# A Mamba block and a routed expert layer on one core: placement earlier on VectorE, ranks earlier on TensorE, the last gate product in halves on GpSimd

## The chip, the core and the metric

The kernel runs on one core of one Trainium2 chip. The metric is the device time of one execution in microseconds (us). Engines are called as in the profile: PE is TensorE (its weight loads are PEld), DVE is VectorE, ACT is ScalarE, POOL is GpSimd, SP is SyncE, which here only issues DMAs.

## The reference

Input x is (2, 2048, 256) in float32, so 4096 tokens of width 256. Two layers follow each other, each with a residual and a layer normalization without scale.

```python
# layer 1: Mamba block without the scan
xz = x @ W_in.T                      # 256 -> 2 * 512: xs, z
xc = silu(causal_depthwise_conv(xs, 4 taps) + conv_b)
dt = xc @ W_x[0:32].T                # 512 -> 32
a  = softplus(dt @ W_dt.T + b_dt)    # 32 -> 512
x  = layernorm(x + (xc * a * silu(z)) @ W_out.T + x)
# layer 2: 16 experts, 4 of them for each token, and a shared expert
scores = sigmoid(x @ gate_w.T); sfc = scores + gate_bias
groups of 4 experts, each rated by its two best sfc; the best 2 of 4 groups stay
topk = the 4 best experts by sfc in the groups that stay
w = 2.5 * scores[topk] / sum(scores[topk])
y = sum over topk of w * (silu(x @ Wg.T) * (x @ Wu.T)) @ Wd.T
y = y + (silu(x @ Ws_g.T) * (x @ Ws_u.T)) @ Ws_d.T
out = layernorm(x + x + y)
```

## The kernel before

**Stages.** The tokens are cut into 8 token tiles of 512. The first stage (to about 300 us of the trace) works through them in a software pipeline. While token tile t has its softplus, output projection and normalization, tile t + 1 has its input projection and convolution, tile t - 1 its gate, routing and shared expert, and tile t - 2 its placement. The second stage (300 to 513 us) runs the experts over 143 list tiles of 128 rows, in 36 groups of four ("quads"). The tail adds the four weighted expert rows of each token and normalizes.

**How a token reaches its experts.** For each token tile DVE finds the four experts of each token (`choose_...`, result `sel`). PE counts, with triangular and all-ones matrices, the rank of each token in each expert's list (`ranks`). DVE then places the tokens: `place_rank` adds the ranks to the counts of the tiles before (two additions), `place_rows` masks them, `place_top` (four MAX8) collects the four positions of each token, and `place_ids` writes the row numbers `row_id` and raises the semaphore `routed`. POOL then sends the rows of the tile to `x_buf` in HBM with indirect DMAs (`send`): four blocks of 128 tokens with four DMAs each, 16 for a token tile. In the second stage SP loads list tiles from `x_buf`, and POOL sends the results to `y_buf` (`send_results`), four indirect DMAs for each quad. POOL works in the order of its program, so the result sends stand behind all row sends.

**POOL's other work.** `gate_product` multiplies the convolved channels `xc` by `silu(z)` for the four chunks of 128 channels of a token tile, into `m`. DVE multiplies `m` by the softplus in halves of two chunks (`softplus_product`), which PE's output projection (`out_proj_by_pairs`) waits for.

**The order on DVE.** All engines run orders that are written out by hand. In `tile(t)` the small routing and placement operations stand between larger ones. `conv_tap(n, c, d)` is one tap of the convolution of chunk c of tile n = t + 1, some 510 columns wide; the taps of one chunk follow each other, each waiting for the one before. `conv_halo(n, i)` adds the columns that reach into the tile before, for chunks 2i and 2i + 1; ACT's `silu_xc` waits for it. The last token tile (t = 7, with p = 5 placed and r = 6 routed) has an order of its own behind the loop, since it has no next tile: no taps, and the table of the first half's list tiles (`table_mm` on PE, `table_out` on DVE). There DVE finishes the weights of token tile 5 first (`weigh_chosen` is the multiplication at line 1688, `slot_chosen` the scan at line 1692, each with two inputs in SBUF), then adds up the gate's logits of tile 6 (`gate_logits`, line 1566, semaphore `gate_sum`).

**Waits that matter.** On PE `ranks(t, logits_read)` waits for `sel_done` of its tile, for `routed` of the tile before it, and for `gate_sum`, because its output shares PSUM bank 3 with the logits that `gate_logits` reads. `place_rank` waits for the ranks. `softplus_sum(7, 0)` waits for ACT's logarithm. `gate_product(7, ...)` waits on POOL for `norm_ready`, which DVE raises at line 1527 (`norm_shift`). SP's load of the expert weights (`load_gu`) waits for all of `m` and stands behind the loads of the first two quads.

Of the kernel before, what the change touches and what calls it, by code (L numbers as in the profile page):

```python
# [22 lines left out]
def mamba_moe(nc, x_tok, x_T, w_in_T, conv_w, conv_b, w_x_T, w_dt_T, b_dt, w_out_T,  # L23
# [9 lines left out]
    SUB = T // P  # L33
    KD, KI, KS = D // P, DI // P, SH // P
# [23 lines left out]
    with ExitStack() as ctx:  # L58
# [539 lines left out]
        def _(pool):  # L598
# [46 lines left out]
            def gate_product(t, chunks):  # L645
                at_least(pool, "wout_mm", 2 * t)
                for c in chunks:
                    at_least(pool, "xc_done", KI * t + c + 1)
                    at_least(pool, "z_evac", KI * t + c + 1)
                    nc.gpsimd.tensor_tensor(m[:, c, :], xc[:, c, :], zs[:, c, :], ALU.mult).then_inc(s["m_done"], 1)  # L650
# [42 lines left out]
            def last_tile(t):  # L693
                send(t - 3, range(1, 2))
                at_least(pool, "norm_ready", t)
                gate_product(t, range(0, KI))
                send(t - 3, range(2, SUB))
                send(t - 2)
                send(t - 1)
                send(t)  # L700
# [30 lines left out]
        def _(pe):  # L731
# [298 lines left out]
            t = NT - 1  # L1030
# [3 lines left out]
            gate_turn(t - 1)  # L1034
            dt_out(t, range(2, KI))
            table_mm(0)
            shared_up(t - 1, 0)
            ranks(t - 2, t)
            out_proj_by_pairs(t)
            shared_up(t - 1, 1)  # L1040
            at_least(pe, "table_done", 2)
# [337 lines left out]
        def _(dve):  # L1379
# [517 lines left out]
            def tile(t, more=True):  # L1897
# [22 lines left out]
                softplus_sum(t, 1)  # L1920
                gate_one(r)
                softplus_product(t, 1)
                gate_score(r)
                conv_tap(n, 1, 1)
                if placed:
                    place_rank(p)
                gate_biased(r)
                conv_tap(n, 1, 2)
                if placed:
                    place_rows(p)  # L1930
                group_pairs(r)
                conv_tap(n, 1, 3)
                if placed:
                    place_top(p)
                group_sums(r)
                conv_halo(n, 0)
                if placed:
                    place_ids(p)
                group_score(r)
                if t < 2:  # L1940
                    weights_low(PIECES_OF[t][0])
                shared_act(r, 0)
# [228 lines left out]
            t = NT - 1  # L2171
# [9 lines left out]
            weights_to_rows(p)  # L2181
            gate_logits(r)
            table_out(0)
            softplus_sum(t, 0)
            softplus_product(t, 0)
            place_rank(p)
            place_rows(p)
            place_top(p)
            softplus_sum(t, 1)
            place_ids(p)  # L2190
            gate_one(r)
            softplus_product(t, 1)
            gate_score(r)
# [148 lines left out]
```

How the kernel before makes its waits and increments, by code:

```python
        def at_least_alone(eng, name, n):  # L237
            if isinstance(n, int):
                return at_least(eng, name, n)
            n = eng.to_reg(n)
            eng.wait_ge(s["ones_ready"], 1)
            eng.wait_ge(s[name], n)
# [1 line left out]
        def at_least(eng, name, n):  # L246
            if isinstance(n, int) and n <= 0:
                return
            eng.wait_ge(s[name], n)
# [346 lines left out]
        @block.gpsimd  # L597
        def _(pool):
            nc.gpsimd.memset(ident[:, :], 0.0).then_inc(s["pool_set"], 1)
            pool.wait_ge(s["pool_set"], 1)
            nc.gpsimd.affine_select(out=ident[:, :], in_=ident[:, :], compare_op=ALU.not_equal, fill=1.0,
                                    base=0, pattern=[[-1, P]], channel_multiplier=1).then_inc(s["id_ready"], 1)
            nc.gpsimd.memset(tri[:, :], 1.0).then_inc(s["pool_set"], 1)
            pool.wait_ge(s["pool_set"], 2)
            nc.gpsimd.affine_select(out=tri[:, :], in_=tri[:, :], compare_op=ALU.is_gt, fill=0.0,
                                    base=0, pattern=[[1, P]], channel_multiplier=-1).then_inc(s["tri_ready"], 1)
            nc.gpsimd.memset(ones[:, :], 1.0).then_inc(s["ones_ready"], 1)
            nc.gpsimd.memset(before[:, :, :], 1.0).then_inc(s["pool_set"], 1)
            pool.wait_ge(s["pool_set"], 3)
            nc.gpsimd.affine_select(out=before[:, :, :], in_=before[:, :, :], compare_op=ALU.is_gt, fill=0.0,
                                    base=0, pattern=[[1, NG], [-1, NG]], channel_multiplier=0) \
```

## Time and profile before

| | us |
|---|---|
| median of 3 runs (lowest to highest) | 550.43 (549.23 to 551.96) |
| the profiled execution's own time | 549.61 |
| its span in the profile | 548.1 |
| PE busy | 516.9 (94%) |
| DVE busy | 412.3 (75%) |
| ACT busy | 376.1 (69%) |
| POOL busy | 327.4 (60%) |

The span is what the trace covers; the rest of the profiled execution's own time (1.5 us) lies around it. Busy shares are means over stages that have different limits. In a timeline row the first number is the start in us from the span's start, the second the time from the first start to the last end of the instructions in the row, and a bracket at its end gives the engine's idle time just before it and what ended it. PE's matmuls overlap, so a row's duration is longer than the step to the next row.

### The profile page before, as it was taken

What the parts mean: (1) busy time and instruction counts of PE and PEld (TensorE: products, weight loads), DVE (VectorE), ACT (ScalarE), POOL (GpSimd) and SP (SyncE); (2) the same over time, 40 slices, a digit from 0 to 9 for tenths busy, and PEclk for the clock granted to TensorE, in tenths of its full rate; (3) what the DMA queues carried; (4) which work ended last, traced back from release to release, by engine and by line L of the source; (5) the groups of instructions that cost most, each with busy time, mean ns of one, the idle gap of its engine ahead of it and who ended that gap; (6) DMA issues with size and microseconds to landing.
All of it is one profiled execution on the core that took longest, in us unless ns stands there. A gap on an engine that the chain in (4) does not pass through costs nothing.

```text
span 548.1 us, 11651 instructions
## 1 busy us (share of the span) xinstructions
PE 516.9 (94%) x3125; PEld 441.7 (81%) x3125; DVE 412.3 (75%) x1097; ACT 376.1 (69%) x961; POOL 327.4 (60%) x361
## 2 busy tenths in 40 slices
PE   5898899999999999999998999999999999999984
PEld 4687486786877868778677899999999999999862
DVE  4887598897997979989796747444354578878964
ACT  4694867949669495692845367778777777777473
POOL 4412013138657486576877777777777777777700
PEclk9999899999999999999999999999999999999996
DMA  6994403224233342312399867986766899997978
GB/s 165 306 260 166 163 38 117 78 83 141 77 140 106 114 142 76 143 65 101 111 328 367 280 223 247 305 257 193 223 197 211 285 301 328 344 320 241 341 234 287
DMA packets 70150, 111.06 MB, mean 203 GB/s; under 512 B 12260, under 2 KB 53477, under 8 KB 69576
## 3 DMA queue, kind: packets, MB, share of 16 engines
q1 hardware_dynamic: 56856, 74.36, 43.3%
q0 software_dynamic: 12672, 35.67, 17.5%
q8 instruction: 29, 0.48, 0.4%
q10 hardware_dynamic: 560, 0.27, 0.2%
q14 instruction: 33, 0.27, 0.2%
HBM read 61.63 MB, written 49.69 MB: 203 GB/s over the span
## 4 chain that ended last, share of the span: by engine, by line
PE 65%; DVE 10%; ACT 7%; DMA 6%; issue 6%; SPq 5%; ACTq 0%; POOL 0%; DVEq 0%; POOLq 0%
PE psum L785 8%; PE psum L726 6%; PE psum L728 6%; PE psum L727 6%; PE psum L760 4%; PE psum L855 4%; DMA tiles_in<-x_buf 4%; PE psum L979 4%; PE psum L981 4%; PE psum L980 4%; PE psum L963 4%; PE psum L1079 3%; SPq L556 2%; PE psum L1003 2%; PE psum L1005 2%
## 5 line engine op out<-in xcount | busy, mean ns | idle before, releaser
L658 POOL DMA_INDIRECT x_buf<-row,row_id x128 | 129.5, 1012 | 51.4 <-issue 35.8
L650 POOL TENSOR_TENSOR m<-xc,zs 128x512 f32<-128x512 f32 x32 | 41.4, 1316 | 93.4 <-DVE shift L1527 55.0
L979 PE MATMUL psum<-ew_gu_hi,t_hi 128*128 x286 | 83.8, 293 | 0.4 <-issue 0.4
L981 PE MATMUL psum<-ew_gu_hi,t_lo 128*128 x286 | 80.9, 283 | 0.0
L980 PE MATMUL psum<-ew_gu_lo,t_hi 128*128 x286 | 80.9, 283 | 0.0
L1449 DVE SCALAR_TENSOR_TENSOR xc<-psum,cw_taps,xc 128x511 f32<-128x511 f32 (+2 forms) x96 | 70.7, 738 | 6.5 <-ACT halo_x L1118 5.1
L715 POOL DMA_INDIRECT y_buf<-y_out,y_ids x56 | 56.9, 1016 | 16.9 <-issue 12.7
L2055 DVE TENSOR_TENSOR e_act<-g_act,psum 128x512 f32<-128x512 f32 x36 | 24.5, 681 | 45.4 <-ACT g_act L1287 41.0
L785 PE MATMUL psum<-wout,m 128*128 128x256 f32 x256 | 57.3, 382 | 1.1 <-DVE m L1484 0.6
L785 PEld LDWEIGHTS psum<-wout,m 128*128 128x128 f32 x256 | 48.0, 190 | 10.0 <-DVE sp L1476 3.1
L726 PE MATMUL psum<-x_hi,win_hi 128*128 128x512 f32 x128 | 53.3, 416 | 2.4 <-issue 1.2
L979 PEld LDWEIGHTS psum<-ew_gu_hi,t_hi 128*128 128x128 f32 x286 | 54.6, 191 | 0.6 <-issue 0.5
L980 PEld LDWEIGHTS psum<-ew_gu_lo,t_hi 128*128 128x128 f32 x286 | 54.8, 192 | 0.0
L981 PEld LDWEIGHTS psum<-ew_gu_hi,t_lo 128*128 128x128 f32 x286 | 54.7, 191 | 0.0
L715 POOL DMA_INDIRECT y_buf<-row,y_ids x40 | 43.3, 1084 | 12.2 <-issue 10.4
L728 PE MATMUL psum<-x_hi,win_lo 128*128 128x512 f32 x128 | 50.3, 393 | 0.0
L727 PE MATMUL psum<-x_lo,win_hi 128*128 128x512 f32 x128 | 50.2, 392 | 0.0
L2046 DVE TENSOR_TENSOR t_lo<-psum,t_hi 128x512 fp32r<-128x512 f32 x72 | 46.3, 683 | 2.3 <-ACT t_hi L1281 2.2
L715 POOL DMA_INDIRECT y_buf<-y_pair,y_ids x40 | 39.5, 987 | 12.2 <-issue 10.7
L1003 PE MATMUL psum<-ew_d_hi,a_hi 128*128 x143 | 43.4, 303 | 1.4 <-ACT y_out L1302 0.6
L2060 DVE TENSOR_TENSOR a_lo<-psum,a_hi 128x512 fp32r<-128x512 f32 x36 | 24.8, 690 | 25.0 <-ACT a_hi L1294 23.7
L1287 ACT ACTIVATE g_act<-psum 128x512 f32<-128x512 f32 x36 | 21.5, 598 | 28.6 <-PE psum L981 28.5
(256 smaller groups left out, 1390.3 us busy)
## 6 DMA issues: line engine op xcount, KB each, us to landing
tiles_in<-x_buf SPq DMA_DIRECT2D x143, 144.0 KB
y_pair<-y_buf SPq DMA_DIRECT2D x20, 512.0 KB
y_in<-y_buf SPq DMA_DIRECT2D x12, 512.0 KB, 7.3
xT<-in_x_T SPq DMA_DIRECT2D x8, 512.0 KB, 4.2
xtok<-in_x_tok SPq DMA_DIRECT2D x8, 512.0 KB, 3.6
gu_hi_buf<-w_hi_now SPq DMA_DIRECT2D x8, 512.0 KB, 3.4
x_buf<-pad_row SPq DMA_DIRECT2D x17, 144.0 KB
raw_gu<-in_wg_T SPq DMA_DIRECT2D x16, 128.0 KB, 3.4
```

The costliest lines, as they stand in the source:

```text
L658: nc.gpsimd.indirect_dma_start(out=x_buf, out_offset=bass.IndirectOffsetOnAxis(ap=row_id[t % ROWS][:, b, k:k + 1], axis=0), in_=row[t % RO ...
L715: nc.gpsimd.indirect_dma_start(out=y_buf, out_offset=bass.IndirectOffsetOnAxis(ap=y_ids[:, q % IDS, i:i + 1], axis=0), in_=y_sent[:, i, :] ...
L726: pe.matmul(o, w_hi, v_hi, start=start, stop=False)
L727: pe.matmul(o, w_hi, v_lo, start=False, stop=False)
L728: return pe.matmul(o, w_lo, v_hi, start=False, stop=stop)
L785: mm = pe.matmul(o, m[:, c, b * P:(b + 1) * P], wout[:, c, :], start=c == 0 and b % 2 == 0, stop=c == KI - 1 and b % 2 == 1)
L979: pe.matmul(o, t_hi[par][:, k, r], w_hi, start=k == 0, stop=False)
L980: pe.matmul(o, t_hi[par][:, k, r], w_lo, start=False, stop=False)
L981: mm = pe.matmul(o, t_lo[par][:, k, r], w_hi, start=False, stop=k == KD - 1)
L1003: pe.matmul(o, a_hi[:, r], w_hi, start=True, stop=False)
L1449: V.scalar_tensor_tensor(xc[:, c, d:T], psum[:, x_bank(c), 0:T - d], taps[:, c, HALO - d:HALO - d + 1], xc[:, c, d:T], ALU.mult, ALU.add). ...
L2046: V.tensor_tensor(t_lo[par][:, k, :], x_turned(q, k), f32(t_hi[par][:, k, :]), ALU.subtract) \
```

## The change

Three orders are changed, and no operation is added or removed. On POOL the last token tile's gate product, four multiplications in a row until now, is cut into two halves, with the four sends of one block of token tile 4 between them. On PE, in the last token tile, the rank matmuls of token tile 5 go ahead of the shared expert's first product. On DVE, in the loop's `tile(t)`, the placement of tile t - 2 no longer alternates with the taps of chunk 1 but with the routing operations ahead of them, and the halo addition follows the third tap. In the last token tile `place_rank` and `place_rows` go ahead of `softplus_sum(7, 0)`, `place_top` between it and `softplus_product(7, 0)`, and `place_ids` behind that product.

```diff
--- before.py
+++ after.py
@@ -693,8 +693,10 @@
             def last_tile(t):
                 send(t - 3, range(1, 2))
                 at_least(pool, "norm_ready", t)
-                gate_product(t, range(0, KI))
-                send(t - 3, range(2, SUB))
+                gate_product(t, range(0, 2))
+                send(t - 3, range(2, 3))
+                gate_product(t, range(2, KI))
+                send(t - 3, range(3, SUB))
                 send(t - 2)
                 send(t - 1)
                 send(t)
@@ -1034,8 +1036,8 @@
             gate_turn(t - 1)
             dt_out(t, range(2, KI))
             table_mm(0)
+            ranks(t - 2, t)
             shared_up(t - 1, 0)
-            ranks(t - 2, t)
             out_proj_by_pairs(t)
             shared_up(t - 1, 1)
             at_least(pe, "table_done", 2)
@@ -1920,23 +1922,23 @@
                 softplus_sum(t, 1)
                 gate_one(r)
                 softplus_product(t, 1)
-                gate_score(r)
-                conv_tap(n, 1, 1)
                 if placed:
                     place_rank(p)
-                gate_biased(r)
-                conv_tap(n, 1, 2)
+                gate_score(r)
                 if placed:
                     place_rows(p)
-                group_pairs(r)
-                conv_tap(n, 1, 3)
+                gate_biased(r)
                 if placed:
                     place_top(p)
-                group_sums(r)
-                conv_halo(n, 0)
+                group_pairs(r)
                 if placed:
                     place_ids(p)
+                conv_tap(n, 1, 1)
+                group_sums(r)
+                conv_tap(n, 1, 2)
                 group_score(r)
+                conv_tap(n, 1, 3)
+                conv_halo(n, 0)
                 if t < 2:
                     weights_low(PIECES_OF[t][0])
                 shared_act(r, 0)
@@ -2181,13 +2183,13 @@
             weights_to_rows(p)
             gate_logits(r)
             table_out(0)
-            softplus_sum(t, 0)
-            softplus_product(t, 0)
             place_rank(p)
             place_rows(p)
+            softplus_sum(t, 0)
             place_top(p)
+            softplus_product(t, 0)
+            place_ids(p)
             softplus_sum(t, 1)
-            place_ids(p)
             gate_one(r)
             softplus_product(t, 1)
             gate_score(r)
```

## Rows read from the trace of the kernel before

**Rows 1.** Busy time by stretch of the trace: start:end, length, busy us (instructions), clock, DMA.

```profile
166.00:200.00 34.00, 34.00 (x154) 26.09 (x153) 29.90 (x91) 23.72 (x44) 22.41 (x26) 1.00 0.34 115
...
340.00:500.00 160.00, 158.03 (x1340) 156.53 (x1340) 96.83 (x170) 122.83 (x443) 123.14 (x122) 1.00 0.82 273
```

**Rows 2.** DVE timeline, token tile 4: start us, us, instruction.

```profile
178.37 0.55 DVE L1575 RECIPROCAL score<-sfc 128x64 f32<-128x64 f32 x1
...
181.89 0.15 DVE L1463 TENSOR_TENSOR xc<-xc,halo 128x6 f32<-128x6 f32 x1
181.97 0.16 DVE L1756 TENSOR_SCALAR row_id<-top 128x16 int32<-128x16 f32 x1
...
191.89 2.31 DVE L1449 SCALAR_TENSOR_TENSOR xc<-psum,cw_taps,xc 128x511 f32<-128x511 f32 x3
```

**Rows 3.** DVE timeline, token tile 6, end of its normalization.

```profile
260.11 0.16 DVE L1527 SCALAR_TENSOR_TENSOR shift<-mv,rstd 128x4 f32<-128x4 f32 x1
```

**Rows 4.** POOL timeline before the last token tile, with idle time before each.

```profile
251.14 0.96 POOL L658 DMA_INDIRECT x_buf<-row,row_id  x1 [1.85 <-DVE row_id L1756]
...
261.00 2.52 POOL L650 TENSOR_TENSOR m<-xc,zs 128x512 f32<-128x512 f32 x2
```

**Rows 5.** POOL timeline, last token tile.

```profile
264.30 2.50 POOL L650 TENSOR_TENSOR m<-xc,zs 128x512 f32<-128x512 f32 x2 [0.77 <-ACT xc L1129]
...
277.98 1.70 POOL L658 DMA_INDIRECT x_buf<-row,row_id  x1 [0.30 <-DVE row_id L1756]
```

**Rows 6.** DVE timeline, token tiles 6 and 7: instructions while POOL multiplies.

```profile
263.13 0.42 DVE L1463 TENSOR_TENSOR xc<-xc,halo 128x6 f32<-128x6 f32 x1
...
266.46 0.39 DVE L1797 SCALAR_TENSOR_TENSOR list_step<-list_size,list_step 128x31 f32<-128x31 f32 x1
```

**Rows 7.** DVE timeline, last token tile.

```profile
268.22 0.68 DVE L1468 TENSOR_TENSOR dt<-psum,dt 32x512 fp32r<-32x512 f32 x1
268.93 0.23 DVE L1688 TENSOR_TENSOR equal<-score,sel 128x64 f32<-128x64 f32 x1
269.08 0.28 DVE L1692 TENSOR_TENSOR_SCAN picked<-ones_f,sel 128x64 f32<-128x64 f32 x1
...
271.60 0.28 DVE L1566 TENSOR_REDUCE score<-psum 128x64 f32<-128x128 f32 x1
...
273.08 1.23 DVE L1476 SCALAR_TENSOR_TENSOR sp<-psum,sp 128x1024 f32<-128x1024 f32 x1 [0.86 <-ACT sp L1149]
274.35 1.22 DVE L1484 TENSOR_TENSOR m<-m,sp 128x1024 f32<-128x1024 f32 x1
275.49 0.22 DVE L1735 TENSOR_TENSOR posn<-psum,counts 128x64 f32<-128x64 f32 x1
...
276.00 0.41 DVE L1752 MAX8 top<-posn 128x8 f32<-128x16 f32 x4
```

**Rows 8.** PE timeline, last token tile.

```profile
271.80 0.50 PE L726 MATMUL psum<-x1T_hi,wsgu_hi 128*128 128x512 f32 x1
...
275.62 7.17 PE L785 MATMUL psum<-wout,m 128*128 128x256 f32 x32 [0.64 <-DVE m L1484]
```

**Rows 9.** SyncE (SP) timeline: the expert weights' load.

```profile
277.76 1.39 SPq L507 DMA_DIRECT2D ew_gu_hi<-gu_hi_buf  x3
```

**Rows 10.** POOL timeline, its last result send.

```profile
519.70 0.99 POOL L715 DMA_INDIRECT y_buf<-row,y_ids  x1 [0.30 <-issue]
```

**Rows 11.** SyncE timeline, loads of the last blocks.

```profile
525.17 2.40 SPq L572 DMA_DIRECT2D y_in<-y_buf  x4
```

**Rows 12.** PE timeline, last sums.

```profile
534.62 5.56 PE L1079 MATMUL psum<-y_in,ident 128*128 128x256 f32 x16 [2.71 <-DVE y_in L2260]
```

**Rows 13.** Busy time by stretch, end of the trace (columns as in group 1).

```profile
534.00:536.00 2.00, 1.38 (x5) 1.22 (x6) 1.76 (x3) 2.00 (x5) 0.00 (x0) 0.87 1.08 385
536.00:538.00 2.00, 2.00 (x6) 1.53 (x6) 0.36 (x2) 1.63 (x4) 0.00 (x0) 0.50 1.09 386
538.00:540.00 2.00, 2.00 (x8) 1.17 (x6) 1.15 (x5) 0.00 (x0) 0.00 (x0) 0.78 1.09 386
```

## The prediction

> **What bounds the kernel now.** I read the busy times by stretch first. In a token tile of the loop PE is busy for 34.00 of 34.00 us, and in the expert stage for 158.03 of 160.00 [rows 1]. So in the loop a gain on DVE or POOL is worth nothing unless PE waits for it. The chain of work that ended last says the same: it runs on PE, except where a token tile hands over. What remains is the last token tile, where the order of the loop ends and PE waits. There I went through the timelines of the four engines side by side, then asked who waits for POOL later on.
>
> POOL is the second candidate, since its sends go on without a gap from the last token tile to its end, and every us that it starts earlier is an us that it ends earlier.
>
> **Placement ahead of the taps (token tiles 2 to 6).** Nothing is added. Before, the row numbers came at 181.97 + 0.16 us, 3.76 us after the reciprocal's start at 178.37 [rows 2]. Three taps lay between; three dependent taps take 2.31 us [rows 2], 0.77 each. With the taps behind, the same small operations, reciprocal included, are through in about 1.6 us (3.76 less 0.7 for each tap's share), so the row numbers come about 2.1 us earlier. The halo addition, at 181.89 before [rows 2], now follows the third tap with nothing between to cover the tap's latency, and two small operations stand ahead of it that stood behind: I take 0.2 us later, bounds 0 and 0.4. In the loop nobody on PE waits for either, so the value is 0. The cover is PE's full 34.00 us: the later halo would show only where it is pushed past PE's need, and no row shows PE idle there.
>
> Where the earlier row numbers do count is POOL's last idle time before the end, 1.85 us at 251.14 [rows 4]. The next 8 sends take 251.14 to 261.00, 1.23 us each [rows 4]. Without the wait they would end 1.6 us earlier, at 259.4. But the gate product behind them waits for the normalization of token tile 6, ready at 260.11 + 0.16, now 0.2 later by the above [rows 3]: POOL multiplies from 260.55 instead of 261.00. What was a wait for row numbers becomes a wait for the normalization.
>
> **The gate product in halves.** The first half takes 2.52 us [rows 4], to 263.1. Four sends, 5.0 us with the gap ahead of them, go to 268.1, and the second half takes 2.5 us [rows 5], from 268.1 to 270.6, where it ran from 264.30 to 266.80 before. The 0.77 us wait for `xc` ahead of it [rows 5] is gone. Who needs the second half? `softplus_product(7, 1)`, which runs behind 276.00 [rows 7], and SP's weight load, which SP reaches at 277.76 [rows 9]. Both are covered, by over 5 us.
>
> The cost is elsewhere. While POOL multiplied, DVE instructions with two inputs in SBUF were held: the halo addition took 0.42 us in place of 0.15 [rows 6, 2] and ended at 263.55, when POOL's product ended (263.52 [rows 4]); the first table instruction took 0.39 and ended at 266.85, POOL's product at 266.80 [rows 6, 5]. The taps, one input in PSUM, were not held: 0.77 each. The Trainium skill says it too (SBUF — State Buffer, Who interferes with whom): a VectorE instruction with two SBUF inputs contends with a GpSimd instruction that reads SBUF, and the loser blocks for the whole instruction. The trace agrees in both instances.
>
> The second half now lies on a stretch of such DVE instructions. `dt_low` starts at 268.22 and has an input in PSUM; the weights of token tile 5 (268.93) and the scan (269.08) have two in SBUF [rows 7]. By my times the multiplication is held to POOL's boundary at 269.3, and the scan behind it to 270.6. It then ends at 270.7 in place of 269.08 + 0.28: d = 1.35 us for all of DVE behind it. Bounds: if the scan slips through with the multiplication at the boundary, d = 0.45; if neither is held, 0. I take 1.35, as both held instructions of the trace were held to the end of POOL's. The 0.27 and 0.2 us that the two old instances cost are given back, which cancels the later halo at this place.
>
> **Ranks and placement in the last token tile.** `gate_logits`, 271.60 to 271.88 [rows 7], moves to 273.2. The ranks on PE wait for it, and the shared product, which started at 271.80 [rows 8] and does not need it, is now queued behind them: PE idles about 1.5 us and starts it at 273.5. It takes 2.9 us and ends at 276.4. On DVE the ranks arrive at 273.65; the additions and the masking issue in the time that they took from 275.49 to 276.00, about 0.4 until the next independent instruction [rows 7]. So `softplus_sum(7, 0)` starts at about 274.05 in place of 273.08. It waited 0.86 us for ACT before [rows 7]; that cover takes about 0.4 of d, and 0.97 remains. Then `place_top`, four MAX8 in 0.41 us [rows 7], stands between sum and product. The product had to wait for the sum anyway, so 0.2 us of it shows, bounds 0 and 0.4. The product moves from 274.35 to 275.5, the output projection from 275.62 [rows 8] to 276.8. That is later than the shared product's 276.4, so the sum is 0.97 + 0.2 = 1.2 us on PE. The old 0.64 us of idle time [rows 8] is the cover of the moved ranks, and it is enough for them alone.
>
> **Behind that.** From the output projection to the first quad PE waits for DVE and ACT, and these for PE, so 1.2 us stays. In the expert stage PE is full [rows 1]. POOL may send token tile 5 when its row numbers come, at about 276.9, in place of 277.98 [rows 5], and ends 1.1 us earlier than 519.70 + 0.99 [rows 10]. SP's last four loads, from 525.17 [rows 11], wait for that. PE waits 2.71 us before its last sums, ended by DVE's addition [rows 12], which comes behind DVE's own normalization, not by a load. So POOL's 1.1 us is worth 0.
>
> **Sum.** 0 + 0 + 0.97 + 0.2 = 1.2 us on 549.61, the profiled execution's own time: 550.8. That execution stood 0.8 below the median, so against the median of 550.43 it is 551.6. A change of 0.5% is 2.75 us, about what a measurement of this kernel can tell from none; 1.2 is 0.2%.
>
> **Rivals.**
> 1. DVE is not held, or slips through at the boundary. With d up to 0.4 the wait for ACT hides it, and only `place_top`'s 0.2 is left: 550.6. For it: POOL's start depends on five small estimates, and 0.8 us earlier would put other instructions under it. Against it: both instances above.
> 2. POOL sets the tail. Then the last loads, 1.1 us earlier, shorten the kernel: 549.3, and less the 1.2 if DVE is held. For it: SP waits for POOL's last sends [rows 10, 11]. Against it: what ends PE's wait [rows 12].
> 3. Slower by over 0.5%: PE's clock falls. The granted clock is 1.00 throughout both stretches of rows 1, but behind the 2.71 us of idle PE [rows 12] it fell to 0.87, 0.50 and 0.78 in three stretches of 2 us [rows 13], the 1.2 GHz level for part of the time. The deficits add up to 0.26 + 1.0 + 0.44 = 1.7 us. PE's new wait before the ranks is 1.5 us. If the clock falls at the output projection as it did there, 1.2 + 1.7 = 2.9 us: 553.3. It decides from an idle time near the 2.71 us on. The Trainium skill (TensorE: Matmul & The Clock Gate, Part 1) states that an idle PE is throttled by default and activity releases it; by that alone the new wait is a risk. Against it: 1.5 us is nearer to the 0.64 us [rows 8], which passed without a fall, than to 2.71.
> 4. The halo and the softplus wait cost more than taken, or POOL's half starts early enough to hold the table rows and so `dt_low`: up to 1.2 us more, 552.8.
>
> **How the numbers follow.** Forecast 0.50; rival 1 0.22; rival 2 0.11; rival 3 0.06; rival 4 0.11. The predicted time is the forecast's, 551.6. The range holds rivals 1 and 4 and the forecast, with half of the runs' spread at each end (549.23 to 551.96): 549.7 to 553.0. Faster by over 0.5% needs 2.75 us, more than rival 2 gives: 0.03. Slower by over 0.5% is rival 3 and the upper end of rival 4: 0.11. Within: 0.86.
>
> **What the profile after would show.** POOL's wait for row numbers in the token tiles gone; its second half of the last gate product near 268.1; the scan of token tile 5 taking over 1 us; PE idle before the ranks of token tile 5 for over 1 us, released by DVE's logits; the last output projection near 276.8; POOL's sends of token tile 5 at about 276.9 and its end near 519.6; the granted clock 1.00 from 270 to 290. Wrong it would be if that scan takes its 0.28 us, if PE's wait before the ranks is under 0.3 us, or if the tail gets shorter with POOL's end.

## The result and the profile after

| | before | after |
|---|---|---|
| median (lowest to highest, runs) | 549.23 (547.28 to 551.96, 9) | 551.85 (548.48 to 554.37, 9) |
| ratio, 95% interval | | 1.0055 [1.0033, 1.0077] |
| profiled execution, its own time | 549.61 | 548.48 |
| its span | 548.1 | 546.9 |

The changed kernel is slower by 0.55%, 2.6 to 3.0 us, just past the 0.5% that a measurement can tell from nothing. The 550.43 in front was the median of three runs of before; nine gave 549.23. The profiled execution of the changed kernel was the fastest of its nine, so spans can't be compared; what the change costs has to be read from distances inside each trace. The expert stage of the changed kernel, by the busy times by stretch (start:end, length, TensorE's busy us, clock, DMA share, GB/s):

```profile
340.00:500.00 160.00, 159.78 (x1362) 1.00 0.84 274
```

In the expert stage this execution lost 0.22 us of PE where the one of before lost 1.97 [rows 1]; no instruction of that stage was changed. The first expert product, before and after, is still 2.77 us later after the change:

```profile
298.87 0.38 PE L979 MATMUL psum<-ew_gu_hi,t_hi 128*128 x1 [0.36 <-issue]
```

```profile
301.64 0.38 PE L981 MATMUL psum<-ew_gu_hi,t_hi 128*128 x1 [0.36 <-issue]
```

But the last sums begin at 534.47 against 534.62 [rows 12], so by then the delay is gone from this trace. Part of it is that TensorE waited 0.2 us for loads of list tiles between 300 and 516 us, where it waited 1.8 us before. Of the lead of 1.2 us in the span 1.05 comes behind that: 12.43 us to the end against 13.48. There the granted clock is 1.00 in the three stretches from 534 to 540 us, where before it was 0.87, 0.50 and 0.78 [rows 13].

The last token tile on VectorE after (lines of before plus 2):

```profile
260.82 0.16 DVE L1529 SCALAR_TENSOR_TENSOR shift<-mv,rstd 128x4 f32<-128x4 f32 x1
...
263.85 0.17 DVE L1465 TENSOR_TENSOR xc<-xc,halo 128x6 f32<-128x6 f32 x1
...
266.92 0.18 DVE L1799 SCALAR_TENSOR_TENSOR list_step<-list_size,list_step 128x31 f32<-128x31 f32 x1
...
268.22 2.87 DVE L1806 SCALAR_TENSOR_TENSOR tile_row<-tile_no,tile_row 128x1 f32<-128x1 f32 x1
271.12 0.68 DVE L1470 TENSOR_TENSOR dt<-psum,dt 32x512 fp32r<-32x512 f32 x1
271.84 0.23 DVE L1690 TENSOR_TENSOR equal<-score,sel 128x64 f32<-128x64 f32 x1
271.98 0.28 DVE L1694 TENSOR_TENSOR_SCAN picked<-ones_f,sel 128x64 f32<-128x64 f32 x1
...
274.50 0.28 DVE L1568 TENSOR_REDUCE score<-psum 128x64 f32<-128x128 f32 x1
...
275.66 1.22 DVE L1478 SCALAR_TENSOR_TENSOR sp<-psum,sp 128x1024 f32<-128x1024 f32 x1
276.79 0.40 DVE L1754 MAX8 top<-posn 128x8 f32<-128x16 f32 x4
277.10 1.21 DVE L1486 TENSOR_TENSOR m<-m,sp 128x1024 f32<-128x1024 f32 x1
```

GpSimd in the same stretch:

```profile
261.07 2.52 POOL L650 TENSOR_TENSOR m<-xc,zs 128x512 f32<-128x512 f32 x2 [1.04 <-DVE shift L1529]
...
268.56 2.50 POOL L650 TENSOR_TENSOR m<-xc,zs 128x512 f32<-128x512 f32 x2
...
278.67 0.96 POOL L658 DMA_INDIRECT x_buf<-row,row_id  x1 [2.64 <-DVE row_id L1758]
```

And the rows with idle time on TensorE:

```profile
271.86 0.73 PE L775 MATMUL psum<-dt,wdt 98*128 98x512 f32 x2 [1.97 <-DVE dt L1470]
274.93 0.20 PE L838 MATMUL psum<-sel,tri 128*128 128x80 bf16 x1 [0.18 <-DVE score L1568]
278.37 7.17 PE L787 MATMUL psum<-wout,m 128*128 128x256 f32 x32 [0.25 <-DVE m L1486]
```

The row to see is L1806. It adds one element per partition and took 2.87 us. It ended at 271.09, with GpSimd's second half at 271.06. `dt_low` (L1470) is queued behind it, TensorE waited 1.97 us for it, and everything up to the expert stage came later. From `norm_shift` to the output projection it is 278.37 - 260.82 = 17.55 us, against 15.51 before [rows 3, 8]: 2.04 us more.

The second loss is not in the last tile. From the logits' sum to `norm_shift` of token tile 1, in the trace of before and in that after:

```profile
67.50 0.28 DVE L1566 TENSOR_REDUCE score<-psum 128x64 f32<-128x128 f32 x1
87.25 0.16 DVE L1527 SCALAR_TENSOR_TENSOR shift<-mv,rstd 128x4 f32<-128x4 f32 x1
```

```profile
67.76 0.28 DVE L1568 TENSOR_REDUCE score<-psum 128x64 f32<-128x128 f32 x1
87.97 0.16 DVE L1529 SCALAR_TENSOR_TENSOR shift<-mv,rstd 128x4 f32<-128x4 f32 x1
```

19.75 us became 20.21. In token tile 1 nothing is placed yet, so the new order leaves the routing chain alone with its latencies, which the taps had covered. And TensorE is not full there: in both traces it waits for VectorE's `x_lo` at the end of that tile (first before, then after), so the 0.46 us goes on: from that logits' sum to `norm_shift` of the last tile it is 260.11 - 67.50 = 192.61 us before and 260.82 - 67.76 = 193.06 after.

```profile
96.88 0.50 PE L726 MATMUL psum<-x_hi,win_hi 128*128 128x512 f32 x1 [1.15 <-DVE x_lo L1494]
```

```profile
97.59 0.50 PE L728 MATMUL psum<-x_hi,win_hi 128*128 128x512 f32 x1 [1.17 <-DVE x_lo L1496]
```

2.04 + 0.46 = 2.50 us, 0.46% of 549.23, inside the measured interval of 0.33 to 0.77%. The agreement doesn't show that this delay is what the runs lost, since the trace doesn't carry it to the end. With the 0.26 us by which this execution was already later at the logits' sum of token tile 1 it makes up the 2.77 us at the first expert product, and no more is shown.

### The profile page after: what moved, and what is told of

Its sections match the earlier page's. It is cut to its first block, busy times and chain, and to the rows that moved or that the text cites. A ratio compares the mean times of both kernels' runs of the same rounds, so it can differ in the third digit from the quotient of the medians.

```text
span 546.9 us, 11652 instructions
## 1 busy us (share of the span) xinstructions
PE 513.8 (94%) x3125; PEld 440.1 (80%) x3125; DVE 415.7 (76%) x1097; ACT 376.1 (69%) x961; POOL 327.0 (60%) x361
## 4 chain that ended last, share of the span: by engine, by line
PE 68%; DVE 16%; ACT 6%; issue 5%; DMA 2%; SPq 1%; POOL 0%; ACTq 0%; DVEq 0%; POOLq 0%
PE psum L787 7%; PE psum L728 6%; PE psum L981 5%; PE psum L982 5%; PE psum L983 5%; PE psum L730 5%; PE psum L729 5%; PE psum L965 5%; PE psum L857 4%; DVE xc L1451 4%; PE psum L1005 3%; PE psum L762 3%; PE psum L1006 3%; PE psum L1007 3%; PE psum L991 3%
## 5 line engine op out<-in xcount | busy, mean ns | idle before, releaser
L658 POOL DMA_INDIRECT x_buf<-row,row_id x128 | 127.5, 996 | 45.2 <-issue 36.2
L717 POOL DMA_INDIRECT y_buf<-y_out,y_ids x56 | 59.2, 1057 | 17.0 <-issue 13.3
```

Of the source, the lines that this page charges most:

```text
L658: nc.gpsimd.indirect_dma_start(out=x_buf, out_offset=bass.IndirectOffsetOnAxis(ap=row_id[t % ROWS][:, b, k:k + 1], axis=0), in_=row[t % RO ...
L717: nc.gpsimd.indirect_dma_start(out=y_buf, out_offset=bass.IndirectOffsetOnAxis(ap=y_ids[:, q % IDS, i:i + 1], axis=0), in_=y_sent[:, i, :] ...
```

## The experiments

e1 to e4 ran on one chip, five rounds, beside 29 runs of the kernel before (547.96 us, 546.96 to 549.35).

**e1_loop: the loop's order alone.** The kernel before with the new order in `tile(t)` and nothing else:

```diff
-                gate_score(r)
-                conv_tap(n, 1, 1)
                 if placed:
                     place_rank(p)
-                gate_biased(r)
-                conv_tap(n, 1, 2)
+                gate_score(r)
...
+                conv_tap(n, 1, 3)
+                conv_halo(n, 0)
```

> The kernel before with the new order of tile(t) on VectorE alone (token tiles 1 to 6). Theory A (the order costs time only where PE waits for DVE, which is token tile 1, where PE waits 1.15 us for x_lo in the trace before and 1.17 after): the normalization of token tile 1 ends 0.45 to 0.5 us later than before, PE's projection behind it too, nothing more in the later tiles; ratio about 1.001 (+0.5 us). Rival B (the prediction's: the order costs nothing in the loop): PE's times unchanged up to the last token tile, ratio 1.000. Rival C (the loop's order is the whole loss): ratio 1.005.

Measured 548.12 us (12 runs), ratio 1.0007 [0.9996, 1.0018]. Token tile 1 took 20.20 us between the two rows shown above, the output projection began 15.41 us behind `norm_shift`. So the order costs 0.45 us in that tile and nothing in the last. From one `norm_shift` to the other it is 261.08 - 88.11 = 172.97 us, against 172.86 before, so the tiles between add at most 0.11. The time alone can't tell 0.45 us from none: its interval holds both.

**e2_halves: the halves alone.** The kernel before with GpSimd's gate product in halves:

```diff
-                gate_product(t, range(0, KI))
-                send(t - 3, range(2, SUB))
+                gate_product(t, range(0, 2))
+                send(t - 3, range(2, 3))
+                gate_product(t, range(2, KI))
+                send(t - 3, range(3, SUB))
```

> The kernel before with the last gate product in two halves among the sends, nothing else. Theory A (a DVE instruction with two SBUF inputs is held while POOL multiplies): the last token tile's second half runs near 268.5 to 271.0 of the trace, the table row's last instruction or one just behind it is held to its end, dt_low starts near 271, PE idles about 2 us ahead of its dt product, and the last output projection starts 1.5 to 2.2 us later; ratio 1.003 to 1.004. Rival B (the loss comes from the ranks and placement order): the output projection starts within 0.3 us of before, ratio 1.000.

Measured 549.64 us (6 runs), ratio 1.0040 [1.0024, 1.0056]. Its VectorE rows, the GpSimd rows and TensorE's wait:

```profile
259.73 0.16 DVE L1529 SCALAR_TENSOR_TENSOR shift<-mv,rstd 128x4 f32<-128x4 f32 x1
...
267.37 0.16 DVE L1806 SCALAR_TENSOR_TENSOR tile_row<-tile_no,tile_row 128x1 f32<-128x1 f32 x1
...
268.51 2.23 DVE L1690 TENSOR_TENSOR equal<-score,sel 128x64 f32<-128x64 f32 x1
270.66 0.28 DVE L1694 TENSOR_TENSOR_SCAN picked<-ones_f,sel 128x64 f32<-128x64 f32 x1
```

```profile
260.61 2.52 POOL L650 TENSOR_TENSOR m<-xc,zs 128x512 f32<-128x512 f32 x2
...
268.13 2.52 POOL L650 TENSOR_TENSOR m<-xc,zs 128x512 f32<-128x512 f32 x2
```

```profile
273.19 0.50 PE L728 MATMUL psum<-x1T_hi,wsgu_hi 128*128 128x512 f32 x1 [1.73 <-DVE res L1554]
```

Here the loop has its old order, and GpSimd is still sending when `norm_shift` comes. Its product begins 0.88 us behind `norm_shift`, where it begins 0.25 behind it after the change. So the table row's last instruction begins 0.76 us ahead of the second half instead of 0.34, and gets through. The next instruction with two SBUF inputs is held, the weights' multiplication, to the end of the whole second half. The output projection came 16.50 us behind `norm_shift` (276.23 - 259.73), 0.99 more than before, where I had expected 1.5 to 2.2. TensorE waits 1.73 us for `res`, which is queued behind the held instruction, so a wait at this place doesn't need the ranks ahead of the shared product. By the times the halves alone carry most of the loss.

The 0.99 us is also less than the 1.3 to 3.1 us that the interval gives. Part of the rest stands behind the last sums. The profiled execution's span is 547.9 us, that of e1 546.6; the last sums begin at 534.39 against 534.13, and from there it takes 13.51 us against 12.47, with the granted clock at 0.81, 0.50 and 0.84 from 534 to 540 us, where e1 has 1.00, 1.00 and 0.97. The trace of before has such a slow end too [rows 13], so one execution doesn't tie it to the halves.

**e3_whole: all but the halves.** The changed kernel with `gate_product(t, range(0, KI))` in one piece again:

```diff
-                gate_product(t, range(0, 2))
-                send(t - 3, range(2, 3))
-                gate_product(t, range(2, KI))
-                send(t - 3, range(3, SUB))
+                gate_product(t, range(0, KI))
+                send(t - 3, range(2, SUB))
```

> The changed kernel with the last gate product whole again (POOL's order as before). Theory A (the halves cause the held instruction): no DVE instruction of the last token tile over 1.3 us, dt_low near 268.7, the output projection of the last token tile near 276.3 (0.45 from token tile 1 and 0.2 from place_top over before), ratio to before about 1.001. Rival B (ranks and placement cost it): output projection near 278, ratio 1.004 to 1.005.

Measured 548.29 us (12 runs), ratio 1.0006 [0.9993, 1.0019]. Token tile 1: 20.20 us. The output projection, 15.57 us behind `norm_shift` at 261.33:

```profile
276.90 3.29 PE L785 MATMUL psum<-wout,m 128*128 128x256 f32 x14 [0.58 <-DVE m L1484]
```

The expected 276.3 was missed because `norm_shift` itself stood later; the distance, 15.57 us, is near the 15.7 expected. Two of the three parts together cost 0.45 us in tile 1 and some 0.1 at the end. Against the changed kernel (1.0055, another chip) the halves make the difference again.

**e4_onein: the held instruction with one SBUF tensor as its input.** The changed kernel, the table row's last instruction written with the row as a scalar per partition:

```diff
-                then(V.scalar_tensor_tensor(tile_row[:, :], tile_no[:, :], float(P), tile_row[:, :], ALU.mult, ALU.add))
+                then(V.tensor_scalar(tile_row[:, :], tile_no[:, :], float(P), tile_row[:, 0:1], ALU.mult, ALU.add))
```

> The changed kernel, but the last instruction of the table's rows (tile number times 128 plus tile_row) takes tile_row as a per-partition scalar in place of a second tensor input; the result is the same. Theory A (the number of SBUF tensor inputs decides who is held): this instruction takes its usual 0.2 us at 268.2, dt_low starts near 268.8, and the next ones with two SBUF inputs, the weights of token tile 5 or the scan near 269.5, are held instead until POOL's second half ends near 271.1; the output projection starts near 277.5 to 278 in place of 278.4, ratio 1.003 to 1.005. Rival B (whatever stands there is held, whatever its inputs): this instruction takes over 2 us again.

Measured 550.05 us (12 runs), ratio 1.0042 [1.0026, 1.0058]. VectorE, then GpSimd, then TensorE:

```profile
267.30 0.21 DVE L1806 TENSOR_SCALAR tile_row<-tile_no,tile_row 128x1 f32<-128x1 f32 x1
267.91 0.68 DVE L1470 TENSOR_TENSOR dt<-psum,dt 32x512 fp32r<-32x512 f32 x1 [0.39 <-ACT dt L1136]
268.62 1.67 DVE L1690 TENSOR_TENSOR equal<-score,sel 128x64 f32<-128x64 f32 x1
270.21 0.28 DVE L1694 TENSOR_TENSOR_SCAN picked<-ones_f,sel 128x64 f32<-128x64 f32 x1
```

```profile
267.68 2.52 POOL L650 TENSOR_TENSOR m<-xc,zs 128x512 f32<-128x512 f32 x2
```

```profile
273.16 0.20 PE L838 MATMUL psum<-sel,tri 128*128 128x80 bf16 x1 [1.60 <-DVE score L1568]
276.59 3.72 PE L787 MATMUL psum<-wout,m 128*128 128x256 f32 x16 [0.26 <-DVE m L1486]
```

The table row now passes and the dt product waits no more; the weights' multiplication is held, and TensorE's wait moves to the ranks. This is close to the course that my forecast had described: the logits' sum comes 1.34 us later behind `norm_shift` than before, where I had put 1.35, though by one instruction held over both multiplications and not by two held in turn. The output projection comes 16.69 us behind `norm_shift` (at 259.90), 1.18 more than before, where the changed kernel had 2.04 more. That the operand form let it pass is likely, not certain: it ended 0.17 us before GpSimd's row begins. In the changed kernel it began 0.34 us before GpSimd's row, here 0.38, so its place is the same and its form differs.

**What e1 to e4 show together.** The two kernels with the halves are slower (lower ends 1.0024 and 1.0026), the two without are not (upper ends 1.0018 and 1.0019). That the halves cost the time is shown. How the delay in the last token tile reaches the end is not: in the traces of before, after and e1 to e4 the first expert product lies between 298.87 and 301.64 us, the last sums between 533.98 and 534.62, and the earliest start, that of before, has the latest last sums. One other thing follows the times, the median of the runs' mean granted clock: 0.9925 in e1 and 0.991 in e3, 0.991 in the kernel before, 0.9895 in e4 and 0.9885 in e2.

The other eight runs, of six kernels, were on two chips where the transfers of the expert stage ran at 143 to 156 GB/s, against 273 before [rows 1], and the kernel before took 678.51 us (35 runs) and 679.86 (23 runs). Some instructions also waited several us for something outside the engines' own work. Their times tell no half per cent; of their traces only the stretches free of such waits are used.

**e5_last: TensorE's ranks ahead and VectorE's order in the last tile, alone.**

```diff
-            shared_up(t - 1, 0)
             ranks(t - 2, t)
+            shared_up(t - 1, 0)
...
-            softplus_sum(t, 0)
-            softplus_product(t, 0)
             place_rank(p)
             place_rows(p)
+            softplus_sum(t, 0)
             place_top(p)
+            softplus_product(t, 0)
+            place_ids(p)
             softplus_sum(t, 1)
-            place_ids(p)
```

> The kernel before with two parts of the change: TensorE's ranks ahead of the shared product in the last tile, and VectorE's new order in the last tile. The loop over the token tiles and GpSimd's gate product stay as before. Theory A (the placement costs what stands between the softplus sum and product, and nothing else): the two sums of place_rank at about 272.5 us, the rows' product behind them, softplus sum where ACT lets it start (0.2 to 0.3 us idle), MAX8 of 0.40 between sum and product; out projection 0.2 us later than in the kernel before when counted from norm_shift (15.7 against 15.51 us), ratio 1.000 to 1.001. Theory B (part of the changed kernel's loss is the placement's): out projection 0.7 us or more later from norm_shift, ratio 1.0015 or more. No VectorE instruction of 128x64 or less lasts over 0.5 us in either.

677.07 us (12 runs), ratio 0.9989 [0.9936, 1.0042]. Inconclusive: VectorE waited 5.37 us ahead of the rank sums for something outside, so neither the distance nor the time answers. What this part costs rests on e3 (15.57 us) beside e1 (15.41), 0.16 us.

**e6_loop_not1 and e12_not1_again: the loop's order without token tile 1.** One kernel, run twice: the new order where something is placed, the old one in token tile 1.

```diff
+                if placed:
+                    place_rank(p)
+                    gate_score(r)
...
+                else:
+                    gate_score(r)
+                    conv_tap(n, 1, 1)
+                    gate_biased(r)
...
```

> The kernel before with the new loop order only in token tiles 2 to 6; token tile 1, which places nothing, keeps its order. Theory A (all that the loop order costs is token tile 1): from the logits' sum to norm_shift of token tile 1 19.75 us as before (20.2 with the new order there too), TensorE's wait for x_lo at about 96.9, norm_shift of the last tile within 0.3 us of 260.1, ratio 0.999 to 1.001. Theory B (the order costs in the later tiles, or the 0.45 us came from elsewhere): tile 1 back at 19.75 us but norm_shift of the last tile still at 260.6 or later, ratio as with the whole loop order or above.

> The same kernel as e6_loop_not1, again for its time. Theory A (all that the loop order costs is 0.45 us in token tile 1): ratio 0.999 to 1.001, the sum from the logits to norm_shift in token tile 1 at 19.75 us, and about 0.0008 below the whole loop order's 1.0007, which one run of this kind can only just tell. Theory B: ratio above 1.001.

Ratios 1.0015 [0.9967, 1.0063] and 0.9970 [0.9926, 1.0014]: no answer in time. The traces do answer for token tile 1, 87.63 - 67.87 = 19.76 us and 86.56 - 66.80 = 19.76, the 19.75 of before. So the 0.45 us came from the order in that tile. In e12 the output projection began 276.52 - 261.26 = 15.26 us behind `norm_shift`, with 0.60 us of wait for `m`: this is what that distance is on that chip without the halves. The expected place of `norm_shift` of the last tile, 260.1, was missed by 1.2 to 2.3 us in both; on these chips everything stands later by then. No trace of the kernel before was kept there, so on the later tiles only e1 answers.

**e8_later: the second half one block of sends later.** The changed kernel with

```diff
-                send(t - 3, range(2, 3))
+                send(t - 3, range(2, SUB))
                 gate_product(t, range(2, KI))
-                send(t - 3, range(3, SUB))
```

> The changed kernel with GpSimd's second half of the last gate product one block of sends later (behind block 3's instead of block 2's), so at about 273.5 to 276.0 us. Theory A (VectorE's instruction with two inputs in SBUF that starts inside GpSimd's multiplications is held to their end, whichever it is): the table row's last instruction takes 0.16 and ends before 269, dt product at about 269.3 with TensorE waiting under 0.3 us for it; instead one of the two-input instructions at 273.5 or later (the placement's product of ranks and selection, or the softplus product) ends with GpSimd's second half at about 276, the softplus sum comes behind it, and the out projection begins at 277.5 to 279: no better than the changed kernel, ratio 1.003 to 1.007. Theory B (only the place at 268 is bad, since the table's row is held there): nothing over 0.5 us of 128x64 elements, out projection at 276.9 and ratio 1.000 to 1.002.

676.17 us (12 runs), ratio 0.9944 [0.9888, 0.9999], whose upper end only just excludes no change, beside a spread of 2% over the runs of before; the trace gives no reason for a gain. The expected 1.003 to 1.007 was missed by the time. VectorE and GpSimd:

```profile
270.45 0.16 DVE L1805 SCALAR_TENSOR_TENSOR tile_row<-tile_no,tile_row 128x1 f32<-128x1 f32 x1
...
275.74 2.58 DVE L1711 SCALAR_TENSOR_TENSOR row<-equal,nabove 128x64 f32<-128x64 f32 x1
```

```profile
275.73 2.50 POOL L650 TENSOR_TENSOR m<-xc,zs 128x512 f32<-128x512 f32 x2
```

The table row takes its 0.16 us. Now `weights_to_rows`, 0.22 us elsewhere, is held for exactly GpSimd's second half, and the logits' sum behind it. So it is not the place at 268 that is bad: whichever instruction with two SBUF inputs is met is held.

**e9_gap: a pause between the two multiplications.** The changed kernel with GpSimd waiting for its own first multiplication:

```diff
-                gate_product(t, range(2, KI))
+                gate_product(t, range(2, 3))
+                at_least(pool, "m_done", KI * t + 3)
+                gate_product(t, range(3, KI))
```

> The changed kernel with a wait on GpSimd between the two multiplications of the second half, on the first one's own completion, so that GpSimd pauses between them for something like 0.1 to 0.3 us. Theory A (VectorE gets in at a boundary if GpSimd pauses there, but not between two back-to-back instructions): the table row's last instruction is held to the first multiplication's end, about 1.3 us instead of 2.87, and the dt product's wait falls from 1.97 to about 0.6; a second two-input instruction may be held by the second multiplication. Theory B (once held, it stays held to the end of the group, or the pause is too short): 2.7 to 3.1 us, as in the changed kernel.

One execution, 678.5 us. VectorE, GpSimd, TensorE:

```profile
270.06 1.52 DVE L1808 SCALAR_TENSOR_TENSOR tile_row<-tile_no,tile_row 128x1 f32<-128x1 f32 x1
271.62 0.68 DVE L1472 TENSOR_TENSOR dt<-psum,dt 32x512 fp32r<-32x512 f32 x1
272.34 0.66 DVE L1692 TENSOR_TENSOR equal<-score,sel 128x64 f32<-128x64 f32 x1
```

```profile
270.28 2.63 POOL L650 TENSOR_TENSOR m<-xc,zs 128x512 f32<-128x512 f32 x2
```

```profile
272.36 0.73 PE L777 MATMUL psum<-dt,wdt 98*128 98x512 f32 x2 [0.91 <-DVE dt L1472]
```

GpSimd's two take 2.63 instead of 2.50 us, so the pause is 0.13. It is enough: the table row is held 1.52 us, about to the end of the first multiplication (270.28 + 1.25 = 271.53), and the weights' multiplication from 272.34 to 273.00, to about the end of the second (272.91). The wait for dt falls from 1.97 to 0.91 us. The output projection comes 279.30 - 262.55 = 16.75 us behind `norm_shift`.

**e7_noread: GpSimd only writes.** The changed kernel with the second half's two multiplications replaced by memsets of the same regions; it leaves out the gate product of the last token tile's second chunk pair.

```diff
-                gate_product(t, range(2, KI))
+                for c in range(2, KI):
+                    nc.gpsimd.memset(m[:, c, :], 0.5).then_inc(s["m_done"], 1)
```

> The changed kernel with the two multiplications of GpSimd's second half replaced by two memsets of the same 128x512 regions: GpSimd writes what it wrote and reads nothing (the last token tile's second chunk pair gets a constant, so the output is not the reference's). Theory A (what holds VectorE is two readers of SBUF that need the same way in): the table row's last instruction takes 0.16 to 0.3 us and ends before 269, TensorE waits under 0.4 us at the dt product, out projection at about 276.9. Theory B (any GpSimd instruction on SBUF holds it, a writer too): VectorE's two-input instruction that starts inside the memsets ends with them.

One execution, 674.07 us. VectorE and GpSimd:

```profile
270.00 0.16 DVE L1807 SCALAR_TENSOR_TENSOR tile_row<-tile_no,tile_row 128x1 f32<-128x1 f32 x1
270.33 0.68 DVE L1471 TENSOR_TENSOR dt<-psum,dt 32x512 fp32r<-32x512 f32 x1 [0.17 <-ACT dt L1137]
271.04 0.23 DVE L1691 TENSOR_TENSOR equal<-score,sel 128x64 f32<-128x64 f32 x1
```

```profile
270.19 1.00 POOL L699 MEMSET m<- 128x512 f32 x2
```

The table row began 0.19 us ahead of the first memset and took 0.16; in e9 it began 0.22 us ahead of a multiplication and took 1.52. That speaks for GpSimd's reading as what holds it, but it is one row of one execution. The weights' multiplication began inside the second memset and took its usual 0.23, but it began at 271.04 and the memset ended at 271.19, so a hold of 0.15 us would hardly show. The Trainium skill (SBUF — State Buffer, Who interferes with whom) states the same: a GpSimd instruction that only writes doesn't contend with a two-input VectorE one; this run agrees, with its 0.16 us. The output projection was later than expected (278.75) for a wait of the rank sums, 1.32 us, that other traces don't have.

**e10_best and e11_best_again: what the runs left.** One kernel, run twice: the new loop order without token tile 1, the ranks ahead, GpSimd's product whole, and `place_top` behind the softplus product (the last tile's order against that of the changed kernel):

```diff
             place_rank(p)
             place_rows(p)
             softplus_sum(t, 0)
-            place_top(p)
             softplus_product(t, 0)
+            place_top(p)
+            softplus_sum(t, 1)
             place_ids(p)
-            softplus_sum(t, 1)
```

> What the runs so far leave: the new loop order in token tiles 2 to 6 alone, TensorE's ranks ahead, the last tile's two rank sums and the rows' product ahead of the softplus sum, but MAX8 behind the softplus product; GpSimd's gate product whole. Theory A (the losses were token tile 1, MAX8 between sum and product, and the halves): out projection 15.5 us behind norm_shift with the wait of about 0.6 us for m, ratio 0.999 to 1.001 against the kernel before: no gain either, since ACT's end of the softplus lays down the sum's start. Theory B (the ranks ahead of the shared product gain once their costs are gone): out projection 15.2 us or less behind norm_shift, ratio under 0.9985.

> The same kernel as e10_best, whose transfers in the expert stage ran at about 150 GB/s on that chip, where they ran at 273 before, so that its times could not tell half a per cent. Theory A: out projection 15.3 to 15.5 us behind norm_shift, ratio 0.999 to 1.001. Theory B (the ranks ahead of the shared product gain once their costs are gone): 15.2 us or less, ratio under 0.9985.

Ratios 0.9973 [0.9925, 1.0021] and 0.9969 [0.9925, 1.0013]. Token tile 1 took 19.76 and 19.73 us. The rank sums waited 4.01 and 5.36 us for something outside, so the distance to the output projection can't be read. Both intervals hold no change; e12, with the loop order alone, has the same ratio. A gain is neither shown nor excluded.

## Why the prediction was right, and where it was not

The predicted 551.6 us is near the measured 551.85, but that is luck: the forecast's +1.2 us stood on a median of 550.43, the measured +2.6 on 549.23, so two errors met. The measured loss is more than the 0.5% to which "slower" had 0.11. The kind of loss was right, its size was not. By its own signs the mechanism failed in the changed kernel: the scan took its 0.28 us, and TensorE's wait before the ranks was 0.18. The range's ends don't follow from its words either: half of the runs' spread, 1.37 us, below 550.6 and above 552.8 gives 549.2 to 554.2.

- **Placement ahead of the taps, tiles 2 to 6.** Right. In token tile 4 after, the rows that answer to [rows 2]:

```profile
179.23 0.55 DVE L1577 RECIPROCAL score<-sfc 128x64 f32<-128x64 f32 x1
180.49 0.16 DVE L1758 TENSOR_SCALAR row_id<-top 128x16 int32<-128x16 f32 x1
...
182.94 0.17 DVE L1465 TENSOR_TENSOR xc<-xc,halo 128x6 f32<-128x6 f32 x1
```

  Row numbers 1.42 us after the reciprocal's start in place of 3.76, so 2.3 earlier (I took 2.1); the halo addition 3.71 in place of 3.52, 0.19 later (I took 0.2). TensorE's busy time from 98 to 260 us is 161.55 against 161.54. GpSimd's waits for row numbers from 100 to 262 us went from five with 14.4 us to one of 4.8, which is off "gone", but they became waits for the normalization as said (25.8 against 16.9 us), and were worth 0.
- **Token tile 1.** The failed step: the cost of the loop's order was put at 0, with "TensorE full" as cover, and the term was confined to token tiles 2 to 6. But the loop begins with tile 1, where nothing is placed and TensorE waits for VectorE. Missed: 0.46 us of distance (e1, e3 and, by its absence, e6 and e12).
- **The halves, the mechanism.** Right in kind: the second half lies on two-input instructions and holds one, and the two that were held before are let off (0.17 and 0.18 us for 0.42 and 0.39 [rows 6]). The halves let off only the table instruction (0.18 in e2 too, 0.39 in e1); the halo addition is let off by the loop's order (0.17 in e1, 0.41 in e2), with which GpSimd's product begins and ends earlier.
- **The halves, who is held.** Wrong in the changed kernel, and this failed step weighs most. I had the half start at 268.1, behind the table rows, of which the last began at 267.96 before. The half's place was right: it began 7.74 us behind `norm_shift`, by my times 268.1 - 260.31 = 7.79. The table row's last instruction began 0.34 us ahead of it, farther than the 0.14 of my times, and was held all the same. The premise that failed is that an instruction which begins ahead of GpSimd's row is safe. It is the outcome that rival 4 names (the table rows held and with them `dt_low`; a part of 0.11), without the earlier start that rival 4 gives for it. Being ahead of `dt_low`, it delayed the dt product (1.97 us), for which the forecast had no wait at all. The delay of tile 1 has no part in it, since GpSimd's product waits for `norm_shift` and moves with it. What decided between the changed kernel and e2 was 0.34 or 0.76 us between the two rows, and that difference comes from the loop's order: with it GpSimd begins 0.63 us earlier behind `norm_shift`, and the halo addition, no longer held, takes 0.24 us off VectorE. Two parts of the change meet here, which the forecast priced one by one.
- **The halves, how long.** Wrong: "held to POOL's boundary at 269.3, and the scan behind it to 270.6". The first one met is held over both multiplications (2.87, 2.23, 1.67 us), and the scan, which starts once they have ended, was held in none (0.28 us in the changed kernel, e2 and e4). With no pause no instruction got in between them; with one of 0.13 us it did (e9). The Trainium skill (SBUF — State Buffer, Who interferes with whom) has the loser blocked for the whole instruction; the trace goes further, over two of them.
- **The sum.** My 0.97 + 0.2 for the last tile came out as 2.04. Counted from start to start, the dt product came 2.19 us later behind `norm_shift` (271.86 - 260.82, before 268.96 - 260.11), the shared product another 0.37, with the ranks now ahead of it, and the output projection 0.52 less, since the ranks no longer stand there and 0.25 us of the old wait of 0.64 is left. When the table row passes (e4) the distance is 1.18 more than before, and the wait before the ranks 1.60 for my 1.5.
- **Behind the last tile.** The forecast carried its 1.2 us through the expert stage, "PE is full". To the first quad that holds: from the output projection to the first expert product it is 23.25 us before and 23.27 after. Through the expert stage the profiled execution doesn't carry it (2.77 us at its start, none at the last sums).
- **place_top between sum and product.** 0.2 us. In the changed kernel sum to product is 277.10 - 275.66 = 1.44 against 1.27 [rows 7]: 0.17.
- **Rivals.** 1 (not held) fell. 3 (clock) is not settled. In the profiled execution the granted clock is 1.00 behind the 1.97 us of idle TensorE, in all windows from 60 to 500 us. But its mean over the span is 0.994, where the other eight of the changed kernel have 0.982 to 0.987, and the 29 of before beside e1 have 0.986 to 0.993. The difference of the medians, 0.991 - 0.985 over 550 us, is an estimated 3.3 us of deficit, counted as the forecast counts it, as much as the whole loss. No trace of such an execution was kept, so where its clock fell is open. An idle time like this one can go either way: behind 2.65 us of idle TensorE in e12 the clock stayed 1.00, behind 2.64 us in e7 it was 0.82, 0.50 and 0.82 from 292 to 298 us. 2 (POOL sets the tail) has no support: GpSimd's sends of token tile 5 began at 278.67, not 276.9, its last one at 520.84 against 519.70 [rows 10], yet TensorE's last wait kept its 2.71 us, ended by VectorE [rows 12]:

```profile
534.47 2.86 PE L1081 MATMUL psum<-y_in,ident 128*128 128x256 f32 x12 [2.71 <-DVE y_in L2262]
```

Open: by what way the halves' delay reaches the end, and how much of the loss is TensorE's clock; whether TensorE's ranks ahead with `place_top` moved gain anything (e10, e11); and why the table row was held although it began up to 0.34 us before GpSimd's row.

## What to carry to other kernels

A GpSimd operation that reads SBUF is priced by which VectorE instruction with two SBUF inputs it meets first and what is queued behind that one, not by its own slack; moving it by half a us changes the victim and can double the delay (0.99 us in e2, 2.04 in the changed kernel), so such a move is judged with every other shift of the same change in place. Before an order in a loop is priced by its steady state, look at the first turns, where some of what covers a latency is not there yet. And a profiled execution that is among the fastest says nothing on the kernel's time: compare distances between the same two rows, then see whether the delay is still there at the end, and compare the mean granted clock of all runs.

## What the runs showed of the hardware

- Two back-to-back multiplications on GpSimd (1.25 us each) held one tiny VectorE instruction over both: 2.87 us for 128x1 elements, 2.58 for 128x64. A pause of 0.13 us between them was enough to let it in (1.52 us).
- VectorE instructions with one input in PSUM were not held: `dt_low` took 0.68 us beside GpSimd's multiplications in e4 (267.91, GpSimd from 267.68) and e9 (271.62 to 272.30, GpSimd to 272.91), as elsewhere.
- A memset of the same region did not hold the table row's instruction that began 0.19 us ahead of it, in one execution.
- A hold can reach back before GpSimd's recorded start: an instruction recorded 0.34 us (0.22 in e9) before GpSimd's row was held, though alone it takes 0.16. At 0.76 us (e2) it was not, nor at 0.38 us when written with one tensor input (e4).
- In 6.14 us of idle TensorE before 282.99 us (e10) the granted clock fell, and it was 0.50 from 280 to 286 us. Behind about 2.65 us it fell once (e7) and stayed once (e12), behind 1.97 us it stayed (the changed kernel).
- A chip on which the expert stage's transfers ran at about 150 GB/s, for 273, ran the kernel before in 678.5 us, where another chip took 548.0. Up to the last `norm_shift` the traces differ little: 261.26 to 263.16 us there, 259.73 to 261.33 on the others.
